# A gated cross-attention block with a routed feed-forward part: the order of the feed-forward steps, the arithmetic of the last product and the place of seven statistics

## What is computed

```python
x = x + tanh(g_xattn) * attention(layernorm(x), ctx)       # 32 heads of 64, 8 groups, 750 context rows
h = layernorm(x)
query = h @ Wq.T                                           # 64 wide
scores = (query @ Wr.T) @ (aux_keys @ Wr.T).T / sqrt(48) + log_rel   # 512 slots
top = top_k(scores, 8)
w = softmax(query @ aux_keys[top].T / 8 + log_rel[top])
z = (w @ aux_values[top]) @ Wvd.T                          # 128 wide
aux = z @ Wvu.T
u = clip(0.5 * log1p(var h) / mean(log1p(var h)) + 2.5 * sigmoid(gelu(h @ Wu1.T + b1) @ Wu2.T + b2), 0, 5)
gate = sigmoid(w1 * clip((u - 0.5) / 1.5, 0, 1) + bias)    # 0 where below 0.05
x = x + tanh(g_ffn) * (h + gate * aux)
```

## Time and profile before

| what | value |
|---|---|
| median of three runs | 1288.43 us |
| the profiled execution, its time | 1289.38 us |
| its span, first to last instruction | 1287.6 us |
| PE busy | 1189.3 us (92%) |
| DVE busy | 983.7 us (76%) |
| ACT busy | 894.4 us (69%) |
| POOL busy | 893.9 us (69%) |
| mean granted TensorE clock | 0.986 of full |

### The profile page before, as it was taken

One profiled execution on the slowest core, in us unless ns is written; L12 is line 12 of the kernel. 1 busy time (PEld: TensorE's weight loads), 2 busy tenths in 40 slices (PEclk: granted clock), 3 DMA queues, 4 the chain that ended last, 5 costly groups with the idle time before them and its releaser, 6 DMA issues.

```text
span 1287.6 us, 34874 instructions
## 1 busy us (share of the span) xinstructions
PE 1189.3 (92%) x14357; PEld 921.2 (72%) x14608; DVE 983.7 (76%) x2206; ACT 894.4 (69%) x1221; POOL 893.9 (69%) x845
## 2 busy tenths in 40 slices
PE   1999999999999999999999999999799998999985
PEld 0888888888888888888888888888475554444442
DVE  3897898899889889988988988888647774555543
ACT  2888888888888888888888888888214345334332
POOL 1899999999999998999999999999200013322221
PEclk9999999999999999999999999999799998999998
DMA  7312222132131213213122211220362000112112
GB/s 265 129 51 72 59 82 72 45 99 78 38 97 41 77 52 92 72 50 93 38 83 57 75 50 45 63 56 15 93 240 101 1 1 1 66 66 86 78 66 98
DMA packets 60080, 94.68 MB, mean 74 GB/s; under 512 B 35666, under 2 KB 44882, under 8 KB 55572
## 3 DMA queue, kind: packets, MB, share of 16 engines
q1 hardware_dynamic: 59492, 89.86, 22.0%
q10 hardware_dynamic: 432, 2.59, 0.5%
HBM read 71.35 MB, written 20.97 MB: 72 GB/s over the span
## 4 chain that ended last, share of the span: by engine, by line
PE 76%; ACT 9%; POOL 5%; DVE 5%; issue 2%; DMA 2%; SPq 0%; POOLq 0%; DVEq 0%
PE psum L744 12%; PE psum L721 11%; PE psum L841 10%; PE psum L751 7%; PE psum L732 6%; PE psum L774 5%; PE psum L768 5%; PE psum L769 5%; PE psum L825 4%; POOL arena L502 4%; PE psum L784 2%; PE psum L853 2%; PE psum L703 2%; ACT arena L607 2%; ACT arena L603 2%
## 5 line engine op out<-in xcount | busy, mean ns | idle before, releaser
L502 POOL TENSOR_TENSOR arena<-arena 128x768 bf16<-128x768 f32 x448 | 651.4, 1467 | 62.2 <-ACT arena L603 43.1
L994 DVE CUSTOM_DVE_ANT_0 arena<-psum,arena 128x750 f32<-128x750 f32 x448 | 420.2, 938 | 99.2 <-PE psum L732 91.1
L607 ACT ACTIVATE arena<-arena,neg_max 128x750 f32<-128x750 f32 x448 | 411.0, 917 | 59.8 <-DVE neg_max L994 59.7
L603 ACT ACTIVATE arena<-psum 128x768 f32<-128x768 f32 x320 | 258.0, 806 | 69.5 <-PE psum L751 67.3
L744 PE MATMUL psum<-ident,arena 128*128 128x128 f32 x1792 | 268.4, 272 | 0.0
L721 PE MATMUL psum<-arena 128*128 128x512 bf16 x675 | 222.1, 383 | 15.7 <-DVE arena L1009 1.6
L768 PEld LDWEIGHTS psum<-arena 128*128 128x128 bf16 (+1 forms) x2688 | 195.3, 98 | 57.4
L769 PE MATMUL psum<-arena 128*128 128x64 bf16 (+1 forms) x2688 | 222.6, 193 | 0.0
L768 PE MATMUL psum<-arena 128*128 128x65 bf16 (+1 forms) x2688 | 222.3, 194 | 0.0
L769 PEld LDWEIGHTS psum<-arena 128*128 128x128 bf16 (+1 forms) x2688 | 179.1, 98 | 53.2
L744 PEld LDWEIGHTS psum<-ident,arena 128*128 128x128 f32 x1792 | 206.0, 140 | 4.4
(11 more groups left out here) (133 smaller groups left out, 1387.4 us busy)
## 6 DMA issues: line engine op xcount, KB each, us to landing
arena<-in_k_t SPq DMA_DIRECT2D x128, 187.5 KB, 3.3
out<-arena SPq DMA_DIRECT2D x14, 1024.0 KB, 3.8
arena<-in_v_rows SPq DMA_DIRECT2D x64, 192.0 KB, 2.4
arena<-in_x_top SPq DMA_DIRECT2D x7, 1024.0 KB, 6.5
arena<-in_x_rest SPq DMA_DIRECT2D x8, 768.0 KB, 4.8
spill<-arena SPq DMA_DIRECT2D x96, 64.0 KB, 2.2
arena<-spill SPq DMA_DIRECT2D x6, 1024.0 KB, 8.4
arena<-in_w_t SPq DMA_DIRECT2D x4, 1024.0 KB, 13.1
```

What stands on the lines that cost most here:

```text
L502: pool.tensor_tensor(p_lo[:, n % RING, :], p_sb[:, n % RING, :], high(p_sb[:, n % RING, :]), ALU.subtract).then_inc(p_split, 1)
L603: act.activation(p_sb[:, n % RING, :], flat_ps[:, turned_at(n):turned_at(n) + CW], ACT.Copy).then_inc(evac_a, 1)
L607: act.activation(s_sb[:, n % RING, 0:CTX], s_sb[:, n % RING, 0:CTX], ACT.Exp, bias=neg_max[:, n % 4, :], scale=-1.0).then_inc(exped, 1)
L994: dve.tensor_tensor_reduce(s_sb[:, n % RING, 0:CTX], flat_ps[:, score_at(n):score_at(n) + CTX], mask_sb[:, max(n % UNITS - REP + 1, 0), :] ...
```

## The change

`sum_half` becomes `sum_wide` (the same matmuls, with a semaphore each quarter, always into bank 2). In a step the queries of quarters 0 to 2 stand ahead of the first wide quarter, and that of quarter 3 ahead of the second. The product of query and Wr goes: the table `rk_aug` is multiplied by Wr once more at the start (`wr_rows`), so that one float32 product of `q_aug` gives the scores. Routing (`route`), `select` and the exp of tile t run in step t, the weights' transposes and z in step t + 1. A result part is three bf16 matmuls, with z split by ACT and DVE and Wvu split by POOL. Seven tiles have their statistics in the attention stage, at the units of `TOP_STATS2`. Tiles end from step 6 on, two in each of steps 6 to 9, one in each of 10 to 13 with its four parts spread over the step, and two at the end in banks of their own. `turn_w`, `sum_z`, `route`, `query_lo`, `gelu`, `weigh`, `copy_w` and `round_z` hold the instructions that stood in the loops before. The last store is in two halves. The old loops of PE, ACT and DVE are removed.

```diff
-V2_TURNS = {(0, 2): range(0, 2), (0, 3): range(2, 4), (1, 0): range(4, 6), (1, 1): range(6, 8)}
-STATS_AT = {2: (0, 1), 3: (0, 3), 4: (1, 1), 5: (1, 3), 6: (2, 1), 7: (2, 3), 8: (3, 1), 9: (3, 3), 10: (4, 1), 11: (4, 3), 12: (5, 1), 13: (5, 3)}
-LOG_STEP = 6
-FIRST_FINISH = 8
-FINISH = {8: (0, 1), 9: (2, 3), 10: (4, 5), 11: (6, 7), 12: (8, 9), 13: (10,), 14: (11,), 15: (12, 13)}
-GATES = (range(0, 6), range(6, 8), range(8, 9), range(9, 10), range(10, 11), range(11, 12), range(12, 13), range(13, 14))
+STATS_AT = {7: (0, 1), 8: (1, 1), 9: (1, 3), 10: (2, 1), 11: (2, 3), 12: (3, 1), 13: (3, 3)}
+TOP_STATS2 = {(4, 5): 0, (5, 2): 1, (5, 5): 2, (6, 2): 3}
+EARLY = BATCH - 1
+LOG_STEP = 4
+FINISH = {6: (0, 1), 7: (2, 3), 8: (4, 5), 9: (6, 7), 10: (8,), 11: (9,), 12: (10,), 13: (11,), 14: (12, 13)}
+GATES = (range(0, 5), range(5, 7), range(7, 8), range(8, 9), range(9, 10), range(10, 11), range(11, 12), range(12, 13), range(13, 14))
...
+    sp.dma_start(wvu, wvu_t).then_inc(wvu_loaded, 16)
+    sp.wait_ge(scored, NU)
...
     for i in range(STAGE_SLOTS):
-        sp.dma_start(av_stage[:, i], av_t[i]).then_inc(v2_loaded[i], 16)
-        sp.dma_start(wvd_stage[:, i], wvd_t[i]).then_inc(v2_loaded[i], 16)
+        load_piece(i)
+    spill_rest(BATCH - 1)
     sp.wait_ge(spilled[(BATCH - 1) % 3], 16 * REP * NB * ((BATCH - 1) // 3 + 1))
-    for i in range(3):
-        sp.dma_start(x2b[:, i, :], spill[128 * i:128 * i + 128]).then_inc(x2_loaded[i], 16)
...
         sp.wait_ge(v2_piece, i - STAGE_SLOTS + 1)
...
+        load_piece(i)
+        if i - STAGE_SLOTS in (0, 2, 4):
+            u = (i - STAGE_SLOTS) // 2
+            sp.dma_start(x2b[:, u, :], spill[128 * u:128 * u + 128]).then_inc(x2_loaded[u], 16)
...
         sp.dma_start(x2b[:, i, :], spill[128 * i:128 * i + 128]).then_inc(x2_loaded[i], 16)
-    sp.dma_start(wvu, wvu_t).then_inc(wvu_loaded, 16)
-    for u in ORDER:
+    for u in ORDER[:-1]:
         sp.wait_ge(y_added, parts_before(u, 4))
         sp.dma_start(out[u], rows_of(u)).then_inc(out_stored, 16)
...
+    for n in range(2):
+        sp.wait_ge(y_added, parts_before(u, 2 * n + 2))
+        sp.dma_start(out[u, :, 1024 * n:1024 * n + 1024], rows_of(u)[:, 1024 * n:1024 * n + 1024]).then_inc(out_stored, 16)
...
-        if k == NU - 4:
-            root2(0)
+        if window == GROUPS - 2 and m == 4:
+            root2(0, EARLY)
...
-    for t in range(1, TILES):
-        root2(t)
+    for t in range(EARLY, TILES):
+        root2(t, t + 1)
...
+    pool.wait_ge(wvu_loaded, 16)
+    pool.tensor_tensor(wvu_lo, wvu, high(wvu), ALU.subtract).then_inc(wvu_split, 1)
...
-        small(pool.tensor_scalar(gb[:, cols], ga[:, cols], 2.5, None, ALU.mult))
+        small(pool.tensor_scalar(gb[:, cols], ga[:, cols], 2.5 / (TAU_HIGH - TAU_LOW), None, ALU.mult))
         small(pool.tensor_tensor(ga[:, cols], gb[:, cols], norm_var[:, cols], ALU.add))
-        small(pool.tensor_scalar(gb[:, cols], ga[:, cols], 0.0, 5.0, ALU.max, ALU.min))
-        small(pool.tensor_scalar(ga[:, cols], gb[:, cols], TAU_LOW, 1.0 / (TAU_HIGH - TAU_LOW), ALU.subtract, ALU.mult))
...
+    round_h(0, 2)
+    round_h(0, 3)
+    round_h(1, 0)
+    act.wait_ge(rk_summed, 1)
+    act.wait_ge(spilled[(BATCH - 3) % 3], 16 * REP * NB * ((BATCH - 3) // 3 + 1))
+    act.activation(g_rows[0:RDIM, :], psum[0:RDIM, 5, :], ACT.Copy, scale=float(RDIM) ** -0.5).then_inc(rk_ready, 1)
...
+    round_h(1, 1)
+    act.wait_ge(route_summed, 1)
+    act.activation(rk_aug[0:BOT, :], psum[0:BOT, 4, :], ACT.Copy).then_inc(tables_ready, 1)
+    round_h(1, 2)
+    query_lo(0)
+    for t in range(1, TILES):
+        if t + 1 <= TILES:
+            round_h(t, 3)
+        if t == 1:
+            act.wait_ge(v2_piece, KC // 2)
+            act.activation(v2, psum[:, 6, :].rearrange("p (m n) -> p m n", m=4), ACT.Copy).then_inc(v2_ready, 1)
+        gelu(t - 1)
+        if t == 1:
+            weigh(0)
+        if t + 1 < TILES:
+            round_h(t + 1, 0)
+        if t == LOG_STEP:
+            act.wait_ge(log_in_done, 1)
+            act.activation(log_var[:, :], log_var[:, :], ACT.Ln, bias=1.0).then_inc(log_var_done, 1)
+        copy_w(t - 1)
+        query_lo(t)
+        bases = FINISH.get(t + 1, ())
+        if bases:
+            base(bases[0])
+        if t + 1 < TILES:
+            round_h(t + 1, 1)
+        if t == 1:
+            act.wait_ge(spilled[(BATCH - 1) % 3], 16 * REP * NB * ((BATCH - 1) // 3 + 1))
+        round_z(t - 1)
+        if len(bases) > 1:
+            base(bases[1])
+        if t + 1 < TILES:
+            round_h(t + 1, 2)
+        weigh(t)
+    gelu(TILES - 1)
+    copy_w(TILES - 1)
+    round_z(TILES - 1)
...
+                pe.wait_ge(w1_split, 4 * j + 4)
+            if j == 0 and t >= 1:
+                pe.wait_ge(preact_done, t)
...
+            for n, (h, w) in enumerate(((h_hi, high(w1_raw[:, k, :])), (h_hi, w1_lo[:, k, :]), (h_lo, high(w1_raw[:, k, :])))):
+                mm = pe.matmul(psum[:, 2, :], h[:, j, kk, :], w, start=(k == 0 and n == 0), stop=(k == KC - 1 and n == 2))
+        if 1 in halves:
+            mm.then_inc(w1_quarter, 1)
...
-        if k >= NU - 2:
-            turn_h(0, k - (NU - 2))
         if k >= 0:
             value(k)
+        if k in (NU - 4, NU - 3):
+            turn_h(0, k - (NU - 4))
+        if k == NU - 2:
+            sum_wide(0, 0)
...
+            pe.wait_ge(wvu_split, 1)
             pe.wait_ge(mean_scaled, 1)
         if n == 0:
+            pe.wait_ge(z_split, u + 1)
+        bank = TAIL_BANKS.get((u, n), 7)
+        if bank == 7 and parts_before(u, n) >= 1:
+            last = parts_before(TILES - 2, 1) if (u, n) == (TILES - 1, 3) else parts_before(u, n)
+            pe.wait_ge(y_added, last)
+        elif bank in (0, 1):
...
+        cols = slice(512 * n, 512 * n + 512)
+        for first, (z, w) in enumerate(((0, high(wvu[:, cols])), (0, wvu_lo[:, cols]), (1, high(wvu[:, cols])))):
+            mm = pe.matmul(aux_ps(u, n), z_cat[:, u, z, :], w, start=(first == 0), stop=(first == 2))
+        mm.then_inc(aux_summed, 1)
...
+    turn_h(0, 2)
+    turn_h(0, 3)
+    sum_query(0, 0)
+    turn_h(1, 0)
+    pe.wait_ge(small_loaded, 64)
+    pe.matmul(psum[0:RDIM, 5, :], wr_t[:, :], keys_aug[0:BOT, :], start=True, stop=True).then_inc(rk_summed, 1)
+    sum_wide(0, 1)
+    sum_query(0, 1)
+    turn_h(1, 1)
+    pe.wait_ge(rk_ready, 1)
+    pe.matmul(psum[0:BOT, 4, :], wr_rows[:, :], g_rows[0:RDIM, :], start=True, stop=True).then_inc(route_summed, 1)
+    pe.wait_ge(x_added, GROUPS)
+    sum_v2(range(0, 2))
+    sum_wide(0, 2)
+    sum_query(0, 2)
+    turn_h(1, 2)
+    sum_v2(range(2, 4))
+    sum_wide(0, 3)
+    sum_query(0, 3)
+    turn_h(1, 3)
+    sum_v2(range(4, 6))
+    route(0)
+    sum_v2(range(6, 8))
+    for t in range(1, TILES):
+        last = t == TILES - 1
+        sum_query(t, 0)
+        sum_query(t, 1)
+        sum_query(t, 2)
+        aux_part(t, 0)
+        sum_wide(t, 0)
+        if not last:
+            turn_h(t + 1, 0)
+        aux_part(t, 1)
+        turn_w(t - 1)
+        sum_query(t, 3)
+        sum_wide(t, 1, range(0, 1))
+        aux_part(t, 2)
+        sum_wide(t, 1, range(1, 2))
+        if not last:
+            turn_h(t + 1, 1)
+        aux_part(t, 3)
+        route(t)
+        sum_z(t - 1)
+        sum_wide(t, 2, range(0, 1))
+        aux_part(t, 4)
+        sum_wide(t, 2, range(1, 2))
+        if not last:
+            turn_h(t + 1, 2)
+        aux_part(t, 5)
+        if t == LOG_STEP:
+            pe.wait_ge(log_summed, 1)
+            pe.matmul(psum[:, 7, 0:1], ones[:, :], log_sum[:, 0:1], start=True, stop=True).then_inc(mean_summed, 1)
+        sum_wide(t, 3, range(0, 1))
+        aux_part(t, 6)
+        sum_wide(t, 3, range(1, 2))
+        if not last:
+            turn_h(t + 1, 3)
+        aux_part(t, 7)
+    for i in range(4):
+        if i == 0:
+            turn_w(TILES - 1)
+        aux_part(TILES, i)
+        if i == 1:
+            sum_z(TILES - 1)
+    for i in range(4, 8):
+        aux_part(TILES, i)
...
+                    dve.wait_ge(mv2_done, u)
+            bank_stats(u, c)
...
         if k == NU - 5:
-            stats_of(0)
-        if k == NU - 3:
             stage_h(0, 0)
             stage_h(0, 1)
-        if k == NU - 2:
-            stats_of(1)
+        if k in (NU - 3, NU - 2):
+            split_h(0, k - (NU - 3))
+            stage_h(0, k - (NU - 3) + 2)
...
+        dve.scalar_tensor_tensor(rows, aux_ps(u, n), aux_scale[:, u:u + 1], rows, ALU.mult, ALU.add).then_inc(y_added, 1)
+    def split_z(t):
+        dve.wait_ge(z_ready, t + 1)
+        dve.tensor_tensor(z_cat[:, t, 1, :], psum[:, 6, 0:128], z_cat[:, t, 0, :], ALU.subtract).then_inc(z_split, 1)
...
+    split_h(0, 2)
+    stage_h(1, 0)
+    split_h(0, 3)
+    stage_h(1, 1)
+    split_h(1, 0)
+    stage_h(1, 2)
+    late_stats(0, 1)
+    split_h(1, 1)
+    stage_h(1, 3)
+    split_h(1, 2)
+    stage_h(2, 0)
+    join_query(0)
+    for t in range(1, TILES):
+        preact(t - 1)
```

(58 more changed lines are left out.)

305 lines of the change are left out of this document (118 added, 187 removed).

## The result

The changed kernel takes 1228.97 us, the median of four runs (1227.84 to 1230.28), against 1289.54 for the kernel before in the same comparison: a ratio of 0.9521 over the runs, 95% interval 0.9507 to 0.9535 (the two medians give 0.953). The forecast was 1232. The profiled execution took 1228.12 us with a span of 1226.3, against 1231.0 forecast for the span.

A forecast was written before the change was run, and what follows sets the result against it. PE, busy over 90% in both stages, was the bound, so its idle time counted. Step 13's end at 1207.6, plus 16.8 tail, 5.1 statistics and 1.5 clock, gave span 1231.0; + 1.8 - 0.95: 1232 us, range 1221 to 1250.

The forecast's parts named there:

- Light steps: Feed-forward steps without result parts: 17.4 us once query gap and Wr product go; 18.2 in steps 2 to 4.
- rival D: Feed-forward steps: queries are ahead but another ACT item is late in turn, 13 x 0.93: 1244 us; chance 0.07.
- Heavy steps: Feed-forward steps 6 to 9, eight result parts each: 23.4 us, including 0.7 of waiting for `finish`; four times 93.6.
- Rival B: Steps 6 to 9, one bank 7: PE idles until DVE has added, stays at 27.8, +18: 1250 us; chance 0.14.
- Steps 10 to 12: Feed-forward steps with four result parts each: 20.05 us a step, 60.2 together.
- Statistics in attention: Attention windows 4 to 6: new statistics cost 0.73 us a batch, 7 batches, +5.1; bounds 0 and 19.
- Rival A: Attention windows 4 to 6: DVE has no slack and statistics run serially, +14: 1246 us; chance 0.11.
- Last addition: Behind attention's last maximum: the addition ends at 914.9 instead of 917.3, gain 2.4 us; bounds 0 and 4.
- Start of step 1: Between attention and step 1: new wait of about 2.5 us, then 28.9 of full PE work, start at 945.6.
- The low clock: Behind the new PE wait near 914: the clock may fall once, +1.5 us; bounds 0 and 3.
- Tail: After step 13: tile 13's gate, four `finish` in own banks and the halved last store, 16.8 us in all.
- E: Steps: a PE, DVE, ACT loop stops PE 3 us each step, its clock falls, +72: 1304 us; chance 0.04.

The follow-up runs named there:

- the exp's place: Kernel before, with the exp of the routing moved behind the copy of the query's low half on ACT: 1278.12 us, ratio 0.9911.
- the statistics' order: Changed kernel with late statistics one place earlier or behind the first quarter's addition of the next step: 1225.69 us, ratio 0.9494.
- the float32 run: Changed kernel with each result part as one float32 matmul instead of three bf16 ones, z kept in float32: 1237.66 us, ratio 0.96.
- the kernel with moved statistics: Changed kernel with early statistics at (5,2), (5,5), (6,2), (7,2) instead of (4,5), (5,2), (5,5), (6,2): 1226.03 us, ratio 0.9503.
- the run that filled it: Changed kernel with tile 0's second wide quarter and second query ahead of tile 1's transposes: 1225.87 us, ratio 0.9496.
- The run with the exp first: Changed kernel with the exp of the routing ahead of the rounding of the next tile's third quarter on ACT: 1229.12 us, ratio 0.9529.
- the run with the queries behind: Changed kernel with a step's three queries put back behind its first wide quarter and result part 0: 1237.28 us, ratio 0.9588.

## Why the prediction was right, point by point

- **Light steps.** 17.4 forecast, 17.39 found; 18.2 forecast with statistics, 18.15, 18.15 and 18.40 found. Both causes were shown by taking them away (the exp's place; the statistics' order). To a tenth the agreement is luck: a bare light step is 17.25, which is 0.14 under the sum, and the wait for `preact` costs 0.90 with its start, which is 0.1 over it. Step 1's 0.5 was 0.32. The 0.93 "a step" was read from light steps and holds for the first five only; a heavy step has no such wait, so the sum for it was not hurt, but rival D's 13 x 0.93 should have been 5 x 0.93.
- **Heavy steps.** 23.4 forecast, 23.28 found. The part of 0.67 is shown by the float32 run, and the remaining wait was 0.40 instead of 0.7. Beside the 2.35 some 0.9 of smaller gaps stood in a heavy step before, which the prediction did not name. Rival B is out: the bank 7 is still single, but of 2.35 in one wait 0.40 is left. Steps 10 to 12: 20.05 forecast, 19.92 found. From the start of step 1 to the last bias the trace has 1210.4 - 949.3 = 261.1 against 262.0 forecast.
- **Statistics in attention.** 5.1 forecast, 2.5 found, and this is the first term that was mis-sized. The 0.45 at (4,5) held (0.50 in each of seven batches), but in batches 1 and 2 window 5 gave it back, which was not foreseen. The 0.28 for (5,2) and (5,5) failed in six batches: I read it off windows near the shortest length, 13.4, but window 5 lasted 13.98 or more already and hid them. In the last batch, where it lasted 13.37, it came as read, 0.25. The bound of 0 "if windows 5 and 6 hide theirs" was the true case for the others. Rival A is out.
- **Last addition.** I let two `stage_h` keep the 2.13 that a pair had taken beside POOL, and expected 2.4; the gain behind the last window is 4.1 (17.4 to 13.3). The pair took 1.07, since the split that POOL had under way ended at 907.26, just behind the pair's start at 906.92. In the kernel with moved statistics the pair starts at 905.41, 0.23 behind the start of a POOL split of 1.47, and lasts 1.98; the last addition then ends 14.8 behind the reciprocal, a gain of 2.6, near the forecast. (The Trainium skill, SBUF — State Buffer, Who interferes with whom, says that whichever of the two engines issues first holds their shared ports for its whole instruction. The traces agree: 1.52 of the 1.98 go to the first of that pair, and in the changed kernel the split that POOL starts inside the pair, at 907.60, lasts 1.71 instead of 1.47.) The price of such a pair is where POOL stands when it starts, not a constant; that it was 1.07 here was luck.
- **Start of step 1.** 952.2 forecast on this sum, 949.3 found. The two terms above give 2.6 + 1.7 less; the offset of the first window, 0.8 later, and some 0.6 more work than the 28.9 summed take back the rest. The low clock cost 1.6 in this execution (56.8 less 55.2) where 1.5 was forecast. The wait itself was 2.3 of 2.5, and the run that filled it puts it with its clock at 3.1 by the medians. In other executions the clock's part was nothing or 3.2, so the forecast's bounds of 0 and 3 were apt, and that its 1.5 was met here is luck.
- **Tail.** 16.8 forecast, 15.9 found: 2.7 instead of 3.4 to the first POOL instruction, 7.3 for the chain instead of 7.0, 2.8 for four `finish`, 3.05 for the store instead of 3.4.
- **The sum.** Start -2.9, steps -0.9, tail -0.9: 4.7 under the forecast span of 1231.0. The median is only 3.0 under the forecast: I took it 0.95 below the profiled execution, as before, and it lies 0.85 above. So the nearness of the total is in part luck: the largest misses, -2.6 in attention and -1.7 behind it, are met by +0.8 for the offset, +0.6 for the work and +1.8 between the profiled execution and the median.
- **Rivals D and E.** The run with the exp first shows slack for most of the delay where I expected the loop to close, and the run with the queries behind shows how far E is: with a stop of 2.1 us in each of three steps, one of them lost 1.6 more to the clock. In the changed kernel the granted clock over 956 to 1206 is 1.00, with waits up to 0.74. (The Trainium skill, TensorE: Matmul & The Clock Gate, section on psum-queue depth-cycling, says that short idling between groups of matmuls can make the clock swing. The steps of the changed kernel show no such case; the one step with the queries behind is the nearest to it.)
